# Four transformer layers on one core: in the two 16-head stages the transposes follow a group's scores by one step and the products with V by two, where they followed by two and three

## The chip, the cores and the metric

One core of one Trainium2 chip runs the whole program. The metric is the device time of one execution in microseconds (us). The engines are PE (TensorE, matrix products and transposes), DVE (VectorE), ACT (ScalarE), POOL (GpSimd) and SP (SyncE); each works through its own list of instructions in the order of the program, and they hand work over by semaphores. SBUF is the on-chip memory, PSUM the accumulator memory that PE writes to.

## The reference

Four layers, each an attention stage and a feed-forward stage, each followed by `x = layernorm(x + stage(x))`, on an input of 4 batches x 512 tokens x 128 features, all in fp32. The change touches the attention of layer 1 and of layer 2, both with 16 heads of 64 features:

```
# layer 1: 16 query heads, 4 key/value heads (each serves 4 query heads)
scores = einsum('bhqd,bhkd->bhqk', q, k) * 64 ** -0.5 + causal
probs  = softmax(scores);  out = einsum('bhqk,bhkd->bhqd', probs, v);  return out @ Wo.T

# layer 2: 16 heads, one more mask
S   = relu(att[:, 0]), shifted down by one query, without the first key and the diagonal
att = att - cumsum(S over queries)
att = where(keep, att, -inf)      # keep: the ~100 keys with the smallest sum, and the diagonal
y   = softmax(att) @ v;  return y @ W_proj.T + b_proj
```

The other stages (a one-head attention, a ternary gated feed-forward, a squared-relu feed-forward, two mixtures of experts, an attention over channels) are not touched.

## The kernel before

The four batches run in a hardware loop, one after the other; within a batch the eight stages follow each other. `A1` is the 16-head stage of layer 1 and `A2` that of layer 2; both use the same code (`heads_pe`, `heads_act`, `heads_dve`, `heads_pool`).

A stage first fills Q, K and V (L641 to L652). Then it goes through **groups**. A group is 128 queries (tile `i` of 4) and as many pairs of heads as make 512 columns of keys: query tile `i` sees `n = (i + 1) * 128` keys, so a group has one pair at 512 and at 384 keys, two pairs at 256 and four at 128. One head of a group is a **unit**. There are 22 groups in a stage: 8 with 512 keys, 8 with 384, 4 with 256 and 2 with 128. A1 takes the sizes in the order 384, 128, 256, 512, A2 in the order 512, 384, 128, 256.

The loop over `t` (L661, and the same loop on ACT and DVE) starts one group in each step and carries the earlier ones on. One group passes through:

- **scores** on PE (L669) into one of two PSUM buffers `GS`;
- **masks** on DVE (L793), one for each unit: add the mask, take the row minimum of the negated scores, write to one of four SBUF buffers `PRG`;
- **exp** on ACT (L758), one for each unit, with the row sums;
- **reciprocal** of the row sums on DVE (L800). It stands in the step after, behind the masks of the next group;
- **scaling** on POOL (L838), one instruction for each unit;
- **transposes** on PE (L711), of 128 x 128 blocks, into the one PSUM buffer `GX`. Those of a unit wait for its scaling (L708), and the first of a group for the copies that empty `GX` (L702 to L704). They stand `LX` steps behind the scores;
- **copies** out of `GX` into one of two buffers `PT`: in A1 half on ACT (L767) and half on DVE (L811), in A2 all on ACT (L769);
- **products with V** on PE (L727), `LO` steps behind the scores, and the copy of their result (L816 on DVE in A1, L774 on ACT in A2).

When the last group of a query tile is through, `heads_rows` multiplies by the output weights (L695) and the tile's normalization runs in the steps that follow; `self.step` takes the place of that from `LO` too. In A2, DVE also finds the keys to keep for the next query tile, in rounds of MAX8 and MATCH_REPLACE8 (L903 to L910), two rounds for each pair of heads of a step, behind the reciprocal.

So a step of PE is written

```
scores(t)                 # waits for the masks of t - 2
transposes(t - LX)        # waits for the scaling of t - LX and for the copies of the group before it
products with V(t - LO)   # waits for the copies of t - LO
```

Of the kernel before, what the change touches and what calls it, by code (L numbers as in the profile page):

```python
# [57 lines left out]
def transformer(nc, inp, out, last_stage=8):  # L58
    ctx = ExitStack()
    with ctx:  # L60
# [509 lines left out]
        GS = [psum[:, 0:2, :], psum[:, 2:4, :]]  # L570
        GX = psum[:, 4:6, :]
        GO = [psum[:, 6, :], psum[:, 7, :]]
        LX, LO = 2, 3

        class Group:

# [1089 lines left out]
```

## Time and profile before

| | us |
|---|---|
| median of 3 runs | 3670.2 |
| lowest and highest | 3670.17, 3671.58 |
| the profiled execution, its own time | 3670.1 |
| its span, first to last instruction | 3668.5 |
| PE busy | 3156.6 (86%) |
| DVE busy | 2364.9 (64%) |
| ACT busy | 1980.3 (54%) |
| POOL busy | 1393.8 (38%) |

A stage is read best from a stretch of the first batch: the loop over groups of A1 lies between 139 and 217 us, that of A2 between 265 and 371 us. The other three batches repeat them. In the view in order of time a row has the start, the busy time from the first to the last instruction of the row, the engine, the line, the shape, how many instructions were merged, and in brackets the idle time before it and who ended it. PEld rows are the weight loads of PE, which overlap its products. The granted clock is the share of TensorE's full 2.4 GHz that it was given; 0.50 is the lower of its two levels, 1.2 GHz.

### The profile page before, as it was taken

What the parts mean: (1) busy time and instruction counts of PE and PEld (TensorE: products, weight loads), DVE (VectorE), ACT (ScalarE), POOL (GpSimd) and SP (SyncE); (2) the same over time, 40 slices, a digit from 0 to 9 for tenths busy, and PEclk for the clock granted to TensorE, in tenths of its full rate; (3) what the DMA queues carried; (4) which work ended last, traced back from release to release, by engine and by line L of the source; (5) the groups of instructions that cost most, each with busy time, mean ns of one, the idle gap of its engine ahead of it and who ended that gap; (6) DMA issues with size and microseconds to landing.
All of it is one profiled execution on the core that took longest, in us unless ns stands there. A gap on an engine that the chain in (4) does not pass through costs nothing. (4 is left out here: it accounts for less than half of the span.)

```text
span 3668.5 us, 52722 instructions
## 1 busy us (share of the span) xinstructions
PE 3156.6 (86%) x19700; PEld 2207.3 (60%) x19700; DVE 2364.9 (64%) x4289; ACT 1980.3 (54%) x4488; POOL 1393.8 (38%) x1292
## 2 busy tenths in 40 slices
PE   4998998888799898888979889888897988988887
PEld 2556567776365646777536564677743655477773
DVE  3366379994246638999415653999931575499983
ACT  1546267773254528777226442877732654277763
POOL 0223066670031307766004120866501322177740
PEclk9998999999899998999989989999998999999999
DMA  4000100000200010000210001000011000100001
GB/s 131 1 1 1 49 12 1 1 1 24 69 1 1 1 61 1 1 1 1 61 33 1 1 1 61 1 1 1 1 61 33 1 1 10 52 1 1 1 1 63
DMA packets 69372, 68.51 MB, mean 19 GB/s; under 512 B 6077, under 2 KB 49623, under 8 KB 68970
## 3 DMA queue, kind: packets, MB, share of 16 engines
q1 hardware_dynamic: 60288, 56.15, 4.9%
q10 hardware_dynamic: 8810, 8.79, 0.7%
q8 instruction: 162, 2.65, 0.3%
q14 instruction: 112, 0.92, 0.1%
HBM read 63.88 MB, written 1.05 MB: 18 GB/s over the span
## 5 line engine op out<-in xcount | busy, mean ns | idle before, releaser
L1417 POOL TENSOR_TENSOR arena<-arena 128x1536 f32<-128x1536 f32 (+9 forms) x480 | 1020.0, 2155 | 395.6 <-DVE arena L1477 296.5
L1285 PE MATMUL psum<-ident,arena 128*128 128x128 f32 (+7 forms) x7168 | 870.0, 280 | 218.3 <-ACT arena L1386 218.1
L1285 PEld LDWEIGHTS psum<-ident,arena 128*128 128x128 f32 (+7 forms) x7168 | 795.8, 138 | 322.3 <-ACT arena L1386 278.6
L1376 ACT ACTIVATE arena<-arena 128x64 f32<-128x64 f32 (+7 forms) x2048 | 708.4, 486 | 139.4 <-PE psum L1294 139.4
L1477 DVE TENSOR_TENSOR arena<-arena,psum 128x1536 f32<-128x1536 f32 (+9 forms) x480 | 494.9, 1064 | 86.2 <-ACT arena L1386 78.5
L1463 DVE TENSOR_TENSOR arena<-arena,psum 128x1536 f32<-128x1536 f32 (+9 forms) x480 | 494.2, 1063 | 7.8 <-POOL arena L1417 5.8
L449 POOL TENSOR_SCALAR veps<-mv 128x1 f32<-128x1 f32 x128 | 24.7, 193 | 1192.4 <-DVE mv L444 1185.7
L838 POOL TENSOR_SCALAR arena<-arena 128x512 f32<-128x512 f32 (+3 forms) x512 | 265.0, 535 | 544.9 <-DVE arena L800 544.7
L1386 ACT ACTIVATE arena<-arena 128x1536 f32<-128x1536 f32 (+2 forms) x288 | 406.5, 1417 | 114.9 <-DVE arena L1463 114.9
L758 ACT ACTIVATE arena<-arena 128x512 f32<-128x512 f32 (+3 forms) x512 | 282.1, 553 | 209.8 <-DVE arena L793 209.8
L711 PE MATMUL psum<-ident,arena 128*128 128x128 f32 x1280 | 192.7, 294 | 92.9 <-ACT arena L769 63.5
L1063 PE MATMUL psum<-arena,stream 128*128 128x512 f32 x512 | 265.7, 601 | 5.0 <-DVE arena L1184 5.0
L711 PEld LDWEIGHTS psum<-ident,arena 128*128 128x128 f32 x1280 | 147.2, 148 | 191.7 <-ACT arena L769 103.2
L1080 PE MATMUL psum<-arena,stream 128*128 128x512 f32 x512 | 241.2, 595 | 0.0
L1294 PE MATMUL psum<-ident,arena 128*128 128x128 f32 (+7 forms) x2048 | 234.0, 273 | 0.0
L1180 DVE TENSOR_TENSOR arena<-arena,psum 128x512 f32<-128x512 f32 x128 | 88.1, 688 | 215.3 <-PE psum L1080 215.3
L1294 PEld LDWEIGHTS psum<-ident,arena 128*128 128x128 f32 (+7 forms) x2048 | 223.4, 137 | 1.2
L1112 ACT ACTIVATE arena<-psum 128x512 f32<-128x512 f32 x128 | 76.4, 597 | 266.3 <-PE psum L1080 266.3
L1184 DVE TENSOR_TENSOR arena<-arena 128x512 f32<-128x512 f32 x128 | 88.6, 692 | 172.5 <-ACT arena L1114 172.5
L669 PE MATMUL psum<-arena 64*128 64x256 f32 (+3 forms) x1024 | 189.8, 477 | 9.6 <-DVE arena L793 7.7
L793 DVE CUSTOM_DVE_ANT_0 arena<-psum,cmask 128x384 f32<-128x384 f32 (+3 forms) x256 | 112.0, 488 | 119.9 <-PE psum L669 119.9
L727 PE MATMUL psum<-arena 128*64 128x128 f32 x2560 | 186.4, 288 | 0.4
(212 smaller groups left out, 4234.1 us busy)
## 6 DMA issues: line engine op xcount, KB each, us to landing
stream<-in_L_ffn_W SPq DMA_DIRECT2D x160, 256.0 KB, 3.1
arena<-in_L_ffn_h_w SPq DMA_DIRECT2D x8, 1024.0 KB, 8.4
arena<-in_L_ffn_w_w SPq DMA_DIRECT2D x12, 256.0 KB, 4.7
arena<-in_L_ffn_h_w ACTq DMA_DIRECT2D x2, 1024.0 KB
wa<-in_L_attn_W_attn ACTq DMA_DIRECT2D x1, 1536.0 KB
wq<-in_L_attn_Wq ACTq DMA_DIRECT2D x2, 512.0 KB
wo<-in_L_attn_Wo ACTq DMA_DIRECT2D x2, 512.0 KB
x<-in_L_attn_x SPq DMA_DIRECT2D x4, 256.0 KB, 3.7
```

What stands on the lines that cost most here:

```text
L711: last = nc.tensor.transpose(GX[:, half, c:c + P], two(PRG[b % 4])[:, half, c:c + P], ident[:])
L758: nc.scalar.activation(pr, pr, ACT.Exp, bias=nb[:, u:u + 1], scale=-1.0, accum_out=rsum[:, u:u + 1]).then_inc(s["probs"], 1)
L838: nc.gpsimd.tensor_scalar(pr, pr, rinv[:, u:u + 1], 1.0, ALU.mult, ALU.mult).then_inc(s["scaled"], 1)
L1063: nc.tensor.matmul(psO, slot[:, 2 * HID + m * P:2 * HID + (m + 1) * P], HR[n % 3], start=n == 0, stop=top2 and n == NE * NM - 1).then_inc( ...
L1080: nc.tensor.matmul(up_bank(n, j), slot[:, j * HID + m * P:j * HID + (m + 1) * P], XS[e % 2], start=True, stop=True).then_inc(s["up"], 1)
L1285: last = nc.tensor.matmul(ps[ch.half][0:rows, to:to + P], buf[:, c:c + rows], ident[:], start=first, stop=False, is_transpose=True, skip_g ...
L1294: last = nc.tensor.matmul(ps[0][0:rows, 0:P], EA[:, k * NH * OWN:k * NH * OWN + rows], ident[:], start=False, stop=k == HD - 1, is_transpo ...
L1376: nc.scalar.activation(by_key[:, 0:HD - r, j], keys[:, h, 0:HD - r], ACT.Exp, bias=NB[:, j:j + 1], scale=Q3[tt % 2][:, j:j + 1]).then_inc( ...
L1386: nc.scalar.activation(D3[n % 5][:, 0:cols], D3[n % 5][:, 0:cols], ACT.Exp).then_inc(s["e"], 1)
L1417: last = nc.gpsimd.tensor_tensor(of_piece(D3[n % 5], piece), q, keys_on(K3[tt % 2], k, nk, w), ALU.mult)
L1463: last = nc.vector.tensor_tensor(d, d, queries_on(psM[ch.half], ch, piece), ALU.subtract)
L1477: last = nc.vector.tensor_tensor(of_piece(W3[n % 2], piece), of_piece(D3[n % 5], piece), keys_on(psV, k, nk, w), ALU.mult)
```

## The change

Both distances of the loop are made one step shorter. The copies out of `GX` and of the results, the steps of `heads_rows` and of the normalization (`self.step`), and the end of the loop (`A.ng + LO`) take their places from the same two numbers and move with them. Nothing is added or removed; every instruction of a group is the same.

```diff
@@ -570,7 +570,7 @@
         GS = [psum[:, 0:2, :], psum[:, 2:4, :]]
         GX = psum[:, 4:6, :]
         GO = [psum[:, 6, :], psum[:, 7, :]]
-        LX, LO = 2, 3
+        LX, LO = 1, 2
 
         class Group:
```

On PE, at the start of the loop of A1, before the change (`a1_scaled` counts scaled units, `a1_pt` and `a1_pt_dve` the two copies, `a1_masked` masks):

```order
L669 MATMUL psum<-arena 128x384 x3
L669 MATMUL psum<-arena 128x384 [waits a1_masked]
L669 MATMUL psum<-arena 128x384
L711 MATMUL psum<-ident,arena 128x128 [waits a1_scaled]
L711 MATMUL psum<-ident,arena 128x128 x2
L711 MATMUL psum<-ident,arena 128x128 [waits a1_scaled]
L711 MATMUL psum<-ident,arena 128x128 x2
L669 MATMUL psum<-arena 128x384 [waits a1_masked]
```

The same place in the changed kernel:

```order
L669 MATMUL psum<-arena 128x384 x3
L711 MATMUL psum<-ident,arena 128x128 [waits a1_scaled]
L711 MATMUL psum<-ident,arena 128x128 x2
L711 MATMUL psum<-ident,arena 128x128 [waits a1_scaled]
L711 MATMUL psum<-ident,arena 128x128 x2
L669 MATMUL psum<-arena 128x384 [waits a1_masked]
L669 MATMUL psum<-arena 128x384
```

The transposes of the first group stood behind the scores of the third group, and now stand behind those of the second; the scores of the third group follow them.

On DVE, the same stretch of A1, as a difference (`-` before, `+` after; `ISA` rows are the masks and the reads of their minimum):

```order
 L793 ISA arena 128x1
 L800 RECIPROCAL arena<-arena 128x2
-L793 ISA arena<-psum,cmask 128x384
-L793 ISA arena 128x1
-L793 ISA arena<-psum,cmask 128x384
-L793 ISA arena 128x1
-L800 RECIPROCAL arena<-arena 128x2
 L811 COPY arena<-psum 128x384
```

The copy of the first group's transposes came behind the masks of the third group and the reciprocal of the second; it now comes directly behind the reciprocal of the first group, ahead of the third group's masks.

## Rows read from the trace of the kernel before

**Rows 1.** The page, busy time of each engine: share of span, instructions

```profile
PE 3156.6 (86%) x19700; PEld 2207.3 (60%) x19700; DVE 2364.9 (64%) x4289; ACT 1980.3 (54%) x4488; POOL 1393.8 (38%) x1292
```

**Rows 2.** Busy time by stretch (length, busy per engine, granted clock, DMA): A1, A2

```profile
139.00:217.00 78.00, 73.12 (x682) 52.37 (x682) 52.82 (x205) 49.69 (x157) 35.39 (x70) 1.00 0.01 2
264.80:371.00 106.20, 86.04 (x694) 61.49 (x692) 72.08 (x293) 61.64 (x175) 35.31 (x70) 0.86 0.00 1
```

**Rows 3.** Line L711: what ended the idle time before it (us, times)

```profile
  ACT arena L769: 166.7, 118
```

**Rows 4.** In order of time: a step of A1 with 512 keys

```profile
188.39 1.09 PE L711 MATMUL psum<-ident,arena 128*128 128x128 f32 x8
188.51 0.69 DVE L793 CUSTOM_DVE_ANT_0 arena<-psum,cmask 128x512 f32<-128x512 f32 x1 [0.18 <-PE psum L669]
...
189.42 1.09 PE L727 MATMUL psum<-arena 128*64 128x128 f32 x16
...
189.99 1.36 POOL L838 TENSOR_SCALAR arena<-arena 128x512 f32<-128x512 f32 x2 [1.74 <-DVE arena L800]
...
191.62 0.69 DVE L793 CUSTOM_DVE_ANT_0 arena<-psum,cmask 128x512 f32<-128x512 f32 x1 [0.63 <-PE psum L669]
```

**Rows 5.** In order of time: POOL hands the first scaled unit of A1 to PE

```profile
142.63 2.34 POOL L838 TENSOR_SCALAR arena<-arena 128x384 f32<-128x384 f32 x4 [17.14 <-DVE arena L800]
...
143.27 1.12 PE L711 MATMUL psum<-ident,arena 128*128 128x128 f32 x6 [0.84 <-POOL arena L838]
```

**Rows 6.** In order of time: a step of A1 with 384 keys

```profile
147.74 0.56 DVE L793 CUSTOM_DVE_ANT_0 arena<-psum,cmask 128x384 f32<-128x384 f32 x1 [0.55 <-PE psum L669]
...
148.43 0.88 PE L727 MATMUL psum<-arena 128*64 128x128 f32 x12
...
148.96 1.15 POOL L838 TENSOR_SCALAR arena<-arena 128x384 f32<-128x384 f32 x2 [1.31 <-DVE arena L800]
...
150.20 0.56 DVE L793 CUSTOM_DVE_ANT_0 arena<-psum,cmask 128x384 f32<-128x384 f32 x1 [0.55 <-PE psum L669]
```

**Rows 7.** In order of time: from 128 keys to 256 keys in A1

```profile
160.52 0.29 DVE L793 CUSTOM_DVE_ANT_0 arena<-psum,cmask 128x128 f32<-128x128 f32 x1 [0.20 <-PE psum L669]
...
162.50 2.82 POOL L838 TENSOR_SCALAR arena<-arena 128x128 f32<-128x128 f32 x8 [1.59 <-DVE arena L800]
...
164.56 0.42 DVE L793 CUSTOM_DVE_ANT_0 arena<-psum,cmask 128x256 f32<-128x256 f32 x1 [0.77 <-PE psum L669]
```

**Rows 8.** In order of time: a step of A1 with 256 keys

```profile
173.78 0.42 DVE L793 CUSTOM_DVE_ANT_0 arena<-psum,cmask 128x256 f32<-128x256 f32 x1 [2.58 <-PE psum L669]
...
175.43 1.85 POOL L838 TENSOR_SCALAR arena<-arena 128x256 f32<-128x256 f32 x4 [3.68 <-DVE arena L800]
...
176.89 0.42 DVE L793 CUSTOM_DVE_ANT_0 arena<-psum,cmask 128x256 f32<-128x256 f32 x1
```

**Rows 9.** In order of time: masks of A2 with 512, 384 and 128 keys

```profile
286.79 0.69 DVE L793 CUSTOM_DVE_ANT_0 arena<-psum,arena 128x512 f32<-128x512 f32 x1
...
290.57 0.69 DVE L793 CUSTOM_DVE_ANT_0 arena<-psum,arena 128x512 f32<-128x512 f32 x1
...
303.80 0.56 DVE L793 CUSTOM_DVE_ANT_0 arena<-psum,arena 128x384 f32<-128x384 f32 x1 [0.48 <-DVE arena L906]
...
306.66 0.56 DVE L793 CUSTOM_DVE_ANT_0 arena<-psum,arena 128x384 f32<-128x384 f32 x1 [0.45 <-DVE arena L906]
...
323.11 0.29 DVE L793 CUSTOM_DVE_ANT_0 arena<-psum,arena 128x128 f32<-128x128 f32 x1 [1.33 <-issue]
...
332.72 0.29 DVE L793 CUSTOM_DVE_ANT_0 arena<-psum,arena 128x128 f32<-128x128 f32 x1
```

**Rows 10.** Clock: two stretches as in Rows 2, and PE's rows behind long waits

```profile
738.00:752.00 14.00, 8.76 (x77) 7.86 (x75) 13.90 (x13) 13.55 (x29) 7.39 (x5) 1.00 0.00 1
334.00:353.00 19.00, 14.21 (x72) 11.53 (x72) 9.35 (x44) 9.77 (x34) 7.45 (x20) 0.50 0.01 2
...
647.83 2.84 PE L1285 MATMUL psum<-ident,arena 128*128 128x128 f32 x24 [2.23 <-ACT arena L1386]
337.00 1.97 PE L711 MATMUL psum<-ident,arena 128*128 128x128 f32 x8 [6.87 <-ACT arena L769]
```

## Prediction, written before the changed kernel was run

> **What bounds the kernel now.** I read the page's busy times first: PE is busy for 86% of the span [rows 1], so any time that PE stands still in a stretch that it bounds is time of the kernel. Then the two stretches by engine: A1's loop takes 78.0 us with PE busy for 73.1 of them, so PE bounds A1. A2's loop takes 106.2 us, with PE busy for 86.0 and DVE for 72.1 [rows 2]; there the rounds on DVE set the pace in part.
>
> Then the steps in order of time. I measure a step from the first mask of a group to the first mask of the next. In A1 a step with 512 keys takes 191.62 - 188.51 = 3.11 us [rows 4], one with 384 keys 150.20 - 147.74 = 2.46 us [rows 6], one with 256 keys 3.11 us [rows 8], and the step from 128 keys to the next size 4.04 us [rows 7]. In A2 a step with 512 keys takes 3.78 us, with 384 keys 2.86 us, and the first one with 128 keys 9.61 us [rows 9]: DVE has two rounds for each pair of heads there.
>
> What the reader is to see in rows 4: POOL starts to scale a group 1.48 us after the first mask **of the next group** (189.99 - 188.51), since the reciprocal stands behind those masks. So the scaling of a group is done one whole step late, and the transposes on PE stand far enough back to find it ready. Where PE does wait ahead of them, it is for ACT's copy (166.7 us over the whole kernel for L769, [rows 3]), and not for POOL.
>
> **The change, part by part.** No instruction is added or removed. What changes is where PE stands in its list. Written for step t, PE now has scores(t), transposes(t-1), products with V(t-2), scores(t+1). The scaling of t-1 waits for the reciprocal of t-1, which waits on DVE for the masks of t, which wait for scores(t). And scores(t+1) stand behind the transposes of t-1 on PE. That closes a loop over a single step through four engines. Everything queued behind the waiting transposes pays: the products with V, the scores of the next group, thus DVE's next masks, thus ACT's exps. In A1 DVE also waits in its own list for its half of the copies (L811) and the result (L816), but these end ahead of the scores that follow, so they add nothing.
>
> The length of the loop, for 512 keys:
>
> - first mask of t to the start of POOL on t-1: 1.48 us [rows 4];
> - POOL's two units, 1.36 us [rows 4], and the handover to PE. The handover is 143.27 - 142.63 = 0.64 us for a first unit of 2.34 / 4 = 0.585 us, so 0.06 us [rows 5]. Together 1.42 us;
> - the transposes of the first unit run while POOL scales the second. The four of the last unit are left: eight take 189.42 - 188.39 = 1.03 us [rows 4], so 0.13 us each and 0.51 us;
> - products with V and the next scores, up to the next first mask: 191.62 - 189.42 = 2.20 us [rows 4].
>
> The sum is 1.48 + 1.42 + 0.51 + 2.20 = **5.61 us, where a step takes 3.11 us** in A1 (+2.50) and 3.78 us in A2 (+1.83, since DVE's rounds fit into POOL's and PE's part of the loop).
>
> For 384 keys: 148.96 - 147.74 = 1.22; 1.15 + 0.06; three transposes 0.39; 150.20 - 148.43 = 1.77 [rows 6]. Sum 4.59 us: +2.13 in A1, +1.73 in A2 (2.86 now, [rows 9]).
>
> For 256 keys: 175.43 - 173.78 = 1.65; 1.85 + 0.06 [rows 8]; two transposes 0.26; 2.20 as for 512 keys. Sum 6.02 us: +2.91.
>
> For 128 keys: 162.50 - 160.52 = 1.98; 2.82 + 0.06 [rows 7]; one transpose 0.13; about 2.0, between 1.77 and 2.20. Sum 6.99 us: +2.95 over the 4.04 us in A1. In A2 the step takes 9.61 us on DVE alone [rows 9], longer than the loop, so +0; that cover is lost only if the loop grows by 2.6 us.
>
> Sums for one batch. A1: 8 x 2.50 + 8 x 2.13 + 4 x 2.91 + 2 x 2.95 = 54.5, less 2.1 for the first step, which has no group to transpose: **52.4 us**. A2: 8 x 1.83 + 8 x 1.73 + 4 x 2.91 + 0 = 40.1, less 1.8 for the first step: **38.3 us**. The three `heads_rows` blocks are on PE's path now and stay there: 0. The end of a stage has one turn of the loop fewer, but its last group must go through the whole chain in either kernel; I take 0 (bounds: one step of 2.5 us less, or 2.5 us more, for 8 stages 20 us either way). Where PE waits for ACT's copy now [rows 3] it will wait for POOL instead; that wait is inside the old step and so inside the difference.
>
> Four batches: 4 x (52.4 + 38.3) = **363 us**.
>
> **The clock** is the unknown. In the new step PE idles from the end of the scores to the first transposes: 5.61 us less the 3.1 us of its work leaves about 2.3 us in one piece. The trace shows both outcomes. Where bursts of 2.84 us alternate with waits, PE is busy for only 8.76 of 14.0 us and the granted clock stays 1.00; one such wait is 2.23 us long [rows 10]. Behind a wait of 6.87 us the clock was at the lower level (0.50, 1.2 GHz), and it stayed there for 19 us, 14.2 of them with PE busy [rows 10]. A step at the lower clock costs 1.97 instead of 1.09 us for eight transposes [rows 10, 4], nearly double; on the loop, half of the transposes and the 2.20 us of products and scores double, so +0.5 + 1.9 = 2.4 us. A2 has two such low stretches today (its mean is 0.86, [rows 2]); now each step in them pays. I take the row nearest to the new pattern, the recurring wait with clock 1.00, for the bulk, and 4 low steps for each batch (two at the start of A2, two around its 128-key groups): 4 x 4 x 2.4 = 38 us. The ends: 0 low steps (0 us) and half of all 44 steps of a batch (4 x 22 x 2.4 = 211 us).
>
> **Sum.** The profiled execution took 3670.1 us, 1.6 us over its span and 0.1 us from the median of 3670.2 us. 3670.1 + 363 + 38 = 4071 us.
>
> **A rule that is weighed.** The Trainium skill, page "TensorE: Matmul & The Clock Gate", section "HAM oscillation — how this bites in real kernels", describes a kernel with some 2 us of products and a wait of 3 to 5 us for each tile, where the clock falls again in every tile. By that rule, taken to hold for our 2.3 us too, nearly all steps would be low, and the sum would be 3670 + 363 + 4 x 44 x 2.4 = 4455 us. The trace agrees for the long wait [rows 10] and disagrees for the recurring waits of 2.2 us, which are shorter than the page's.
>
> **The rivals.**
>
> *The clock falls in many steps of both stages.* The idle piece of 2.3 us is a little longer than any that the trace shows at clock 1.00, and the steps with 128 and 256 keys have transposes that come one by one behind POOL, which leaves PE nearly idle for longer. For it: A2's stretches at 0.50. Against: the stretch at 738 us. At half of the steps: 3670 + 363 + 211 = 4244 us. Chance 0.24.
>
> *Only A1 pays.* DVE's rounds cover the loop in A2, so that A2 stays at its pace: 3670 + 4 x 52.4 = 3880 us. It would need POOL to be ready within 3.78 us including the products and scores; the legs sum to 5.61. Chance 0.07.
>
> *Not slower.* The transposes of t-1 find their scaling ready, the waits for ACT's copy go, and each stage ends a turn earlier. This decides at one place, the reciprocal on DVE: if it were issued ahead of the masks of the next group, or if those masks and POOL (1.48 + 1.42 us) fit beside PE's own work between two scores. Then the price is 8 stages x one step of 2.5 to 3.1 us less: 3670 - 8 x 2.8 = 3648 us. Against it: the trace shows POOL starting 1.48 us after the next group's mask in every step, and PE has nothing but the waiting transposes in front of it. Chance 0.02. That the change doesn't do what it says (a distance that is also fixed elsewhere) would give 3670 us; the order of the program shows it moved. Chance 0.01.
>
> **How the numbers follow.** The forecast, 4071 us, has 0.66. Its own bounds are the end of the stages (20 us either way) and the low steps (from 0 to about 10 for each batch): 4010 to 4150 us. The range has to reach into the first rival, up to 4240 us, and leaves out the milder cases, for 8 in 10: 3990 to 4240 us. A measurement of this kernel can tell about 0.2% from no change. Faster by more than that: 0.02; within it: 0.01; slower: 0.97.
>
> **What would show it.** In the profile after: PE's idle time ahead of L711 ended by POOL (L838), and hardly by ACT's copies; steps of 5.6 us with 512 keys and 4.6 us with 384 keys in both stages, 6.0 and 7.0 us with 256 and 128 keys; A1's loop near 130 us, A2's near 150 us; all engines' busy times as now but for PE's at the lower clock; the other six stages unchanged. The forecast is wrong if the steps show other lengths at clock 1.00 (a leg is mis-sized), if the granted clock in A1 falls below 0.9 (the first rival), or if A2's steps with 512 keys stay at 3.8 us (the second).

## The result: 605 us slower, and the profile after

The changed kernel takes **4275.1 us** (median of 3 runs, 4272.6 to 4275.3) where the kernel before takes 3670.2 us. The ratio is 1.165, 95% interval 1.162 to 1.167. The forecast was 4071 us with a range up to 4240 us. The direction and the loop of one step hold; the share of the clock does not.

The granted clock over the span in 40 slices (tenths), before:

```profile
PEclk9998999999899998999989989999998999999999
```

The page after, first the busy times and then the same 40 slices:

```profile
PE 3459.5 (81%) x19700; PEld 2385.4 (56%) x19700; DVE 2369.8 (55%) x4289; ACT 2008.0 (47%) x4488; POOL 1391.5 (33%) x1292
...
PEclk9788799999878779999987878999998686899999
```

DVE and POOL are busy for as long as in [rows 1], ACT for 28 us more. PE is busy for 303 us **more** (3459.5 against 3156.6) with the same 19700 products: it ran them slower. The two 16-head stages of the first batch by stretch, which answer to [rows 2] (length, busy times, then the granted clock as the third number from the end):

```profile
141.00:302.00 161.00, 111.82 (x673) 76.05 (x674) 53.78 (x203) 51.81 (x155) 35.20 (x70) 0.71 0.00 1
351.20:526.00 174.80, 120.04 (x710) 82.25 (x708) 72.98 (x296) 66.95 (x179) 36.00 (x72) 0.72 0.00 1
```

A1's loop took 78 us and takes 161, A2's took 106 and takes 175, and the mean clock fell from 1.00 and 0.86 to 0.71 and 0.72. These two differences make 152 us for a batch and 606 us for four: all of the loss of 605 us lies in the two stages.

What ended the idle time ahead of the transposes, after (line L711, us and times), where [rows 3] had ACT's copy:

```profile
  issue: 505.3, 168
  POOL arena L838: 494.1, 411
```

The copy is gone from the list and POOL is there, as the loop of one step demands. This view, like [rows 3], counts the weight loads of PE together with its products, so its times are not PE's lost time. The products alone stand in the page, before and then after:

```profile
L711 PE MATMUL psum<-ident,arena 128*128 128x128 f32 x1280 | 192.7, 294 | 92.9 <-ACT arena L769 63.5
...
L711 PE MATMUL psum<-ident,arena 128*128 128x128 f32 x1280 | 296.2, 378 | 413.0 <-POOL arena L838 412.4
```

They waited 412.4 us for POOL after the change, and 63.5 us (not 166.7) for ACT's copy before it. In order of time, a step of A1 with 384 keys after, to set beside [rows 6]:

```profile
161.35 0.56 DVE L793 CUSTOM_DVE_ANT_0 arena<-psum,cmask 128x384 f32<-128x384 f32 x1 [1.29 <-PE psum L669]
...
162.57 1.15 POOL L838 TENSOR_SCALAR arena<-arena 128x384 f32<-128x384 f32 x2 [5.42 <-DVE arena L800]
...
163.30 1.51 PE L711 MATMUL psum<-ident,arena 128*128 128x128 f32 x6 [2.00 <-POOL arena L838]
...
164.74 1.55 PE L727 MATMUL psum<-arena 128*64 128x128 f32 x12
...
166.22 1.65 PE L669 MATMUL psum<-arena 64*128 64x384 f32 x4
...
167.92 0.56 DVE L793 CUSTOM_DVE_ANT_0 arena<-psum,cmask 128x384 f32<-128x384 f32 x1 [1.29 <-PE psum L669]
```

The loop is readable leg by leg: masks, 1.22 us later POOL, 0.73 us later the transposes (with 2.00 us of idle time on PE before them), the products with V, the next scores, the next masks. The step is 167.92 - 161.35 = 6.57 us, where the sum of legs gave 4.59. The first two legs are as forecast. All the difference is on PE: twelve passes of products take 1.55 us instead of 0.88, the scores 1.65 instead of 0.92. This is the lower of the two clock levels, 1.2 GHz, and it held through this whole stretch (length, busy times, clock 0.50):

```profile
146.00:176.00 30.00, 20.46 (x95) 11.87 (x93) 9.56 (x34) 8.58 (x24) 4.88 (x9) 0.50 0.00 1
```

With 512 keys the clock changes inside each step. A step after, beside [rows 4]:

```profile
283.20 0.69 DVE L793 CUSTOM_DVE_ANT_0 arena<-psum,cmask 128x512 f32<-128x512 f32 x1 [0.77 <-PE psum L669]
...
285.53 1.94 PE L711 MATMUL psum<-ident,arena 128*128 128x128 f32 x8 [2.37 <-POOL arena L838]
...
287.40 1.70 PE L727 MATMUL psum<-arena 128*64 128x128 f32 x16
...
289.03 1.13 PE L669 MATMUL psum<-arena 64*128 64x512 f32 x4
...
290.20 0.69 DVE L793 CUSTOM_DVE_ANT_0 arena<-psum,cmask 128x512 f32<-128x512 f32 x1 [0.77 <-PE psum L669]
```

Behind 2.37 us of idle time the transposes run at the lower level (1.94 us for eight, 1.09 in [rows 4]), and the clock is back for the scores (1.13 us). This step is 7.00 us long. Its neighbours take 7.12 to 7.26 us, and the one that carries the product with the output weights 9.20 us.

### The profile page after: what moved, and what is told of

The parts are those of the page before. It is cut to its first block and busy times, and to the rows that moved or that the text cites. A ratio compares the mean times of both kernels' runs of the same rounds, so it can differ in the third digit from the quotient of the medians.

```text
span 4273.5 us, 52722 instructions
## 1 busy us (share of the span) xinstructions
PE 3459.5 (81%) x19700; PEld 2385.4 (56%) x19700; DVE 2369.8 (55%) x4289; ACT 2008.0 (47%) x4488; POOL 1391.5 (33%) x1292
## 5 line engine op out<-in xcount | busy, mean ns | idle before, releaser
L1285 PE MATMUL psum<-ident,arena 128*128 128x128 f32 (+7 forms) x7168 | 867.4, 279 | 209.4 <-ACT arena L1386 208.2
L1285 PEld LDWEIGHTS psum<-ident,arena 128*128 128x128 f32 (+7 forms) x7168 | 792.0, 137 | 313.7 <-ACT arena L1386 268.0
L711 PE MATMUL psum<-ident,arena 128*128 128x128 f32 x1280 | 296.2, 378 | 413.0 <-POOL arena L838 412.4
L711 PEld LDWEIGHTS psum<-ident,arena 128*128 128x128 f32 x1280 | 193.6, 183 | 590.1 <-issue 505.3
L793 DVE CUSTOM_DVE_ANT_0 arena<-psum,arena 128x512 f32<-128x512 f32 (+3 forms) x256 | 112.6, 488 | 350.5 <-PE psum L669 182.8
L727 PE MATMUL psum<-arena 128*64 128x128 f32 x2560 | 289.7, 397 | 0.4
L727 PEld LDWEIGHTS psum<-arena 128*64 128x64 f32 x2560 | 228.1, 206 | 49.0 <-issue 47.6
L669 PE MATMUL psum<-arena 64*128 64x256 f32 (+3 forms) x1024 | 251.6, 614 | 1.9 <-ACT arena L745 1.9
```

Of the source, the lines that this page charges most:

```text
L711: last = nc.tensor.transpose(GX[:, half, c:c + P], two(PRG[b % 4])[:, half, c:c + P], ident[:])
L727: last = nc.tensor.matmul(bank[half * HD:(half + 1) * HD, j * P:(j + 1) * P], V[:, c:c + HD], pt[:, half, j * g.n + kt * P:j * g.n + (kt + ...
L1285: last = nc.tensor.matmul(ps[ch.half][0:rows, to:to + P], buf[:, c:c + rows], ident[:], start=first, stop=False, is_transpose=True, skip_g ...
```

## The experiments

Two causes are proposed for the loss of 605 us. The first is the **loop of one step**: transposes wait for a scaling that starts behind the next group's masks. The second is the **low clock** that PE's idle piece brings. A rival to the first is that the products with V, or the copies, are what hurts. A rival to the second is that I undersized a leg. Unless said otherwise, each kernel below has the changed distances 1 and 2.

### near_fill: the same loop at the full clock

```diff
+                    fill(pe, A, t, 10)     # 8 for 384 keys; 26, 34, 28 in three long waits of A2
                     heads_transpose(pe, A, t - LX)
...
+        def fill(pe, A, t, times):
+            bank = GO[0]
+            if t >= LO:
+                A.bank_free(pe, "values", t - LO)
+                bank = A.bank("values", t - LO)
+            for _ in range(times):
+                nc.tensor.matmul(bank[:, 0:P], ident[:], ident[:], start=True, stop=True)
```

> The changed kernel (distances 1 and 2) with 128x128 products of the identity put into PE's wait ahead of the transposes, 10 for a step (8 for 384 keys, 26 to 34 where DVE's rounds make the wait long), into the result bank that is free then. They do no work for the output. If the missing 204 us of the forecast are the clock, its steps run at 5.6 us (512 keys) and 4.6 us (384 keys) at a granted clock near 1.00 and the time is the sum of the legs, 3670 + 363 = 4033 us (4000 to 4060). If the steps are long for another reason (a leg that I sized too small), the fill only adds work and the time stays at 4275 us or above.

The idle products go ahead of the transposes, 10 in most steps. Measured: **4042.0 us**, 233 us less than the changed kernel though PE has more to do. The stretches of the two stages:

```profile
141.00:270.00 129.00, 127.87 (x1082) 98.34 (x1079) 53.65 (x203) 50.48 (x154) 35.19 (x70) 1.00 0.01 1
321.00:463.00 142.00, 140.32 (x1205) 112.21 (x1202) 70.40 (x289) 66.04 (x175) 35.27 (x70) 1.00 0.01 1
```

The clock is 1.00 in both, and a step with 512 keys in A1 (here L802 are the masks, L693 the fill, L847 POOL, L720 the transposes, L736 the products):

```profile
247.20 2.50 PE L693 MATMUL psum<-ident 128*128 128x128 f32 x20
247.32 0.69 DVE L802 CUSTOM_DVE_ANT_0 arena<-psum,cmask 128x512 f32<-128x512 f32 x1 [0.51 <-PE psum L669]
...
248.80 1.36 POOL L847 TENSOR_SCALAR arena<-arena 128x512 f32<-128x512 f32 x2 [4.32 <-DVE arena L809]
...
249.64 1.23 PE L720 MATMUL psum<-ident,arena 128*128 128x128 f32 x8
...
250.80 1.09 PE L736 MATMUL psum<-arena 128*64 128x128 f32 x16
...
253.00 0.69 DVE L802 CUSTOM_DVE_ANT_0 arena<-psum,cmask 128x512 f32<-128x512 f32 x1 [0.77 <-PE psum L669]
```

The step is 253.00 - 247.32 = 5.68 us where the sum of legs gave 5.61. With 384 keys it is 4.66 us (4.59), with 256 keys 6.12 (6.02), from 128 keys to the next size in A1 7.08 (6.99). So no sum of legs was more than 0.10 us too small, and filling the waits, which brings the clock to 1.00, is worth 233 us.

### x1_o3 and x2_o2: one distance at a time

Against the kernel before:

```diff
-        LX, LO = 2, 3
+        LX, LO = 1, 3      # x1_o3
+        LX, LO = 2, 2      # x2_o2
```

> Only the transposes one step nearer (distance 1), the products with V at 3 as before. My theory: the loop of a single step is closed by the transposes, which wait for the scaling behind the next group's masks, so nearly the whole loss is here: 4250 to 4300 us, POOL ending PE's waits. Rival: the products with V are what hurts, as they now follow their transposes by one step in a shorter pipeline; then this stays near 3670 us.

Measured: **4259.6 us**. The transposes alone bring 589 of the 605 us, with the same release (line L711, weight loads counted in) and nearly the same clock in A1 as the changed kernel, 0.74 where that has 0.71:

```profile
  POOL arena L838: 503.6, 428
...
141.00:300.00 159.00, 109.21 (x673) 74.72 (x672) 51.68 (x203) 50.60 (x154) 35.17 (x70) 0.74 0.00 1
```

The first steps of this kernel show something else. With 384 keys and the same idle piece of 2.0 us, the transposes ran at the full clock at first and at the lower one later:

```profile
151.69 1.01 PE L711 MATMUL psum<-ident,arena 128*128 128x128 f32 x6 [2.00 <-POOL arena L838]
...
168.53 1.51 PE L711 MATMUL psum<-ident,arena 128*128 128x128 f32 x6 [1.99 <-POOL arena L838]
```

> Only the products with V one step nearer (distance 2), the transposes at 2 as before. The products of a group then stand right behind its own transposes and wait for the copies out of PSUM, which wait for the transposes' end and, on ACT, for the exps of that step. My estimate from the legs: a step with 512 keys becomes masks, exps and the 0.6 to 1.0 us copy, then products and scores, 5.0 us in A1 and 5.4 us in A2: 3960 us at full clock, up to 4030 us with low steps. If only the transposes' distance matters, 3670 us.

Measured: **4052.5 us**, 22 us above the upper figure. A step with 512 keys in A1 is 4.99 us, as estimated. Its wait is another one: the products with V follow their own transposes and wait for ACT's copy, which stands behind that step's exps.

```profile
240.78 0.69 DVE L793 CUSTOM_DVE_ANT_0 arena<-psum,cmask 128x512 f32<-128x512 f32 x1 [0.51 <-PE psum L669]
...
243.58 1.09 PE L727 MATMUL psum<-arena 128*64 128x128 f32 x16 [1.81 <-ACT arena L767]
...
245.78 0.69 DVE L793 CUSTOM_DVE_ANT_0 arena<-psum,cmask 128x512 f32<-128x512 f32 x1 [0.77 <-PE psum L669]
```

The clock was 0.92 in A1's stretch, but 0.79 in A2's (141 to 262 and 313 to 463 us). That this is what I had too small is likely, but no run fills this kernel's waits.

Each distance by itself costs a lot, 589 and 381 us, and together they cost 605. The 381 us are no part of the 605. They come from products that stand in the same step as their own transposes. In the changed kernel the products are one step behind them, as before, and the page has PE waiting 0.4 us in all ahead of L727. So the products' distance, with the transposes already at 1, adds only the last 16 us.

### near_recip_first: the place where the loop closes

```diff
             for t in range(A.ng + LO):
+                if 0 <= t - 1 < A.ng:
+                    g = A.groups[t - 1]
+                    dve.wait_ge(s["probs"], g.end)
+                    nc.vector.reciprocal(rinv[:, g.u0:g.end], rsum[:, g.u0:g.end]).then_inc(s["rinv"], 1)
                 if t < A.ng:
...
-                if 0 <= t - 1 < A.ng:
-                    g = A.groups[t - 1]
-                    dve.wait_ge(s["probs"], g.end)
-                    nc.vector.reciprocal(rinv[:, g.u0:g.end], rsum[:, g.u0:g.end]).then_inc(s["rinv"], 1)
```

> The changed kernel (1 and 2), but on DVE the reciprocal of group t-1 stands ahead of the masks of group t. If the loop is closed through that reciprocal's place behind the next masks, scaling starts before those masks and a step shrinks to about 4 us in A1 and to DVE's 3.8 us in A2 (512 keys): 3790 us (3740 to 3850), clock above 0.9. If the loss came from PE's own order or from the copies, moving the reciprocal does little: above 4150 us.

Measured: **3794.3 us**. Moving one small instruction of DVE gives back 481 of the 605 us, the clock's part included: the mean clock is 0.95 and 0.87 in the two stages (139 to 238 and 285 to 402 us). In A1 with 512 keys (L785 is the reciprocal, L797 the masks):

```profile
214.21 0.13 DVE L785 RECIPROCAL arena<-arena 128x2 f32<-128x2 f32 x1
...
214.64 0.69 DVE L797 CUSTOM_DVE_ANT_0 arena<-psum,cmask 128x512 f32<-128x512 f32 x1 [0.30 <-PE psum L669]
...
215.30 1.36 POOL L838 TENSOR_SCALAR arena<-arena 128x512 f32<-128x512 f32 x2
...
216.14 1.23 PE L711 MATMUL psum<-ident,arena 128*128 128x128 f32 x8 [1.54 <-POOL arena L838]
```

POOL starts 0.66 us after the masks instead of 1.48, and here only that late because it had the normalization's two instructions first; in the next step it starts 0.34 us ahead of them. The remaining 124 us over the kernel before were not taken apart. PE still waits for POOL, 1.54 us in the last row and 150.3 us in all ahead of the products of L711.

### near_fill_small_pool: POOL's leg by itself

Against near_fill; two idle products fewer in most steps go with it, and the kernel leaves out most of the scaling:

```diff
-                        nc.gpsimd.tensor_scalar(pr, pr, rinv[:, u:u + 1], 1.0, ALU.mult, ALU.mult).then_inc(s["scaled"], 1)
+                        nc.gpsimd.tensor_scalar(pr[:, 0:16], pr[:, 0:16], rinv[:, u:u + 1], 1.0, ALU.mult, ALU.mult).then_inc(s["scaled"], 1)
```

> near_fill with POOL scaling only the first 16 columns of each unit, so most probabilities stay unscaled (work left out), and 2 idle products fewer for a step. This measures POOL's leg of the loop. POOL's unit falls from 0.68 us (512 keys) to about 0.26 us; the transposes of the last unit then no longer wait for it. By the sum of legs a step with 512 keys falls by 0.6, with 384 by 0.5, with 256 by 0.8 us, some 25 us for a batch: 3940 us (3920 to 3970). If POOL were not in the loop, the time would stay at near_fill's 4042 us.

Measured: **3943.7 us**, 98 us below near_fill, 3940 expected. POOL's line in near_fill, then in this kernel (busy us, mean ns of one):

```profile
L847 POOL TENSOR_SCALAR arena<-arena 128x512 f32<-128x512 f32 (+3 forms) x512 | 264.1, 532 | 886.8 <-DVE arena L809 886.4
```

```profile
L847 POOL TENSOR_SCALAR arena<-arena 128x16 f32<-128x16 f32 x512 | 133.5, 278 | 912.2 <-DVE arena L809 911.8
```

POOL works 131 us less in all, and 98 of them come off the time, of an engine that is busy for a third of the span. Steps with 512, 384 and 256 keys in A1 are 5.10, 4.19 and 5.31 us, so 0.58, 0.47 and 0.81 us shorter; 0.6, 0.5 and 0.8 were expected.

### near_fill_half and near_fill_2: how much fill the clock needs

Against near_fill, with `times` for its numbers:

```diff
-                    fill(pe, A, t, times)
+                    fill(pe, A, t, times // 2)      # near_fill_half
+                    fill(pe, A, t, times // 4)      # near_fill_2
```

> Distances 1 and 2 with half as many idle products as near_fill (5 for a step, 4 for 384 keys), so that PE's idle piece of a step is about 1.2 us instead of 2.3 us. If the length of the idle piece decides, the clock stays near 1.00 and the time is that of near_fill or a little less, 4035 us. If any recurring idle piece of this kind brings the low clock, it lies between: 4100 to 4200 us.

Measured: **4041.6 us**, the same as with all of the fill, with idle pieces of 1.06 us (512 keys) and 0.91 us (384 keys). The stretches (the second one holds some 28 us around A2 as well):

```profile
141.00:270.00 129.00, 107.07 (x869) 75.63 (x866) 53.62 (x203) 50.43 (x154) 35.38 (x70) 0.99 0.00 1
310.00:480.00 170.00, 142.72 (x1071) 103.19 (x1070) 88.28 (x340) 74.38 (x191) 36.19 (x72) 0.96 0.00 1
```

> Distances 1 and 2 with a quarter of near_fill's idle products (2 for a step), which leaves PE's idle piece at about 1.9 us where near_fill_half left 1.2 us and the changed kernel 2.4 us. near_fill_half kept a clock of 0.96 to 0.99 in these stages. If 1.9 us is short enough, as the recurring waits of 1.5 to 2.2 us in the channel stage are, the time is again 4040 us; if it is already too long, the time lies between 4040 and 4275 us, near 4200 us.

Measured: **4143.2 us**, between. This kernel shows both levels, by size of group. With 384 keys the idle piece is 1.35 us and the clock stays at 1.00; around the groups with 128 keys it is 2.09 us and the transposes run at the lower level (1.51 us for six); with 512 keys it is 1.73 us, and there are steps of both kinds:

```profile
161.24 1.01 PE L720 MATMUL psum<-ident,arena 128*128 128x128 f32 x6 [1.35 <-POOL arena L847]
...
176.21 1.51 PE L720 MATMUL psum<-ident,arena 128*128 128x128 f32 x6 [2.09 <-POOL arena L847]
...
249.63 1.23 PE L720 MATMUL psum<-ident,arena 128*128 128x128 f32 x8 [1.73 <-POOL arena L847]
250.79 1.67 PE L736 MATMUL psum<-arena 128*64 128x128 f32 x16
252.39 2.08 PE L669 MATMUL psum<-arena 64*128 64x512 f32 x4
...
262.52 1.23 PE L720 MATMUL psum<-ident,arena 128*128 128x128 f32 x8 [1.73 <-POOL arena L847]
263.68 1.09 PE L736 MATMUL psum<-arena 128*64 128x128 f32 x16
264.70 1.13 PE L669 MATMUL psum<-arena 64*128 64x512 f32 x4
```

The same piece of 1.73 us is followed by slow scores (2.08 us) once and by fast ones (1.13 us) twelve microseconds later. So the length of the idle piece alone does not decide, as in x1_o3 above; what else does is open. That waits of up to 2.2 us keep the clock, as they do in the channel stage, does not carry over to these stages.

### before_fill and before_fill_long: the kernel before with its own low stretches filled

The diff of before_fill; before_fill_long has 19 in place of the 9, and 3 in the step behind:

```diff
+                    fill(pe, A, t, {2: 14, 17: 5, 18: 29, 19: 9}.get(t, 0) if A is A2 else 0)
                     heads_transpose(pe, A, t - LX)
```

> The kernel before (distances 2 and 3) with 58 of the same idle products in A2 alone: 14 ahead of the first group's transposes, 5, 29 and 9 in the three steps around its 128-key groups, where PE waits for DVE's rounds. If A2's two low stretches cost time there (a delay of the masks by 0.8 us and 5 to 6 us in the rows and steps behind the 128-key groups), each batch gains about 6 us: 3646 us (3640 to 3660). If DVE hides the low clock in A2, nothing changes: 3670 us.

Measured, with 57 idle products and not 58: **3658.8 us**, ratio to the kernel before 0.9967, interval 0.9954 to 0.9979. It is faster, but by half of what was expected. A2's stretch, to set beside [rows 2], where its clock was 0.86:

```profile
264.80:371.00 106.20, 93.74 (x830) 70.47 (x829) 73.88 (x299) 62.23 (x178) 36.07 (x72) 0.98 0.01 1
```

The masks of A2 span 87.3 us instead of 90.4, so 3.2 us for each batch come back and not 6. The 0.8 us at the first groups came as expected (a step of 4.54 us is 3.78). Behind the 128-key groups 2.3 us came (12.00 to 9.67 us), where 5 to 6 were expected.

> before_fill with 19 idle products instead of 9 in the step behind A2's 128-key groups and 3 in the next, since PE still idled for 2.1 us there and the clock fell again. If that low stretch still costs rows and products, another 1 to 3 us for each batch: 3650 us (3645 to 3658). If the longer fill delays the transposes by as much, it stays at 3659 us.

Measured: **3657.5 us**, ratio 0.9963 (0.9948 to 0.9977), not to be told from before_fill. The step that was to gain fell from 9.67 to 8.30 us, but the next one grew from 3.11 to 3.83 us. The clock of A2's stretch is 1.00 now, and the masks span 86.6 us. So all of A2's low clock cost its masks 3.8 us for a batch; where the rest of the expected 6 us was hidden was not looked into.

## Why the prediction was wrong

From the first group's first mask to the last group's first mask of a stage in the first batch, in us, from DVE's rows of each trace:

| | A1 | A2 | sum | x 4 batches, over before |
|---|---|---|---|---|
| before | 65.8 | 90.4 | 156.3 | |
| forecast by the legs | | | 247.0 | 363 |
| near_fill (clock 1.00) | 117.8 | 128.7 | 246.5 | 361 |
| after | 147.9 | 157.8 | 305.7 | 598 |

**What bounds the kernel; the loop: right.** POOL ended PE's waits ahead of the transposes, the masks came 1.22 and 1.49 us before POOL as read from [rows 4, 6], DVE's 128-key steps in A2 stayed at DVE's pace (9.63 us after, 9.61 in [rows 9]), and the channel stage kept its pace (the page has its transposes of L1285 busy for 867.4 us, 870.0 before).

**The legs: right.** 363 us were forecast, 361 us are there at the full clock, and near_fill's time is 371 us above the kernel before. That the two numbers are so close is partly luck. In A2 the steps with 384 keys paid 15.5 us where 13.8 were forecast, those with 256 keys 9.5 where 11.6 were. Of the remaining 10 us, 8 lie between A1's last masks and A2's first: 62.8 us in near_fill, 60.9 before. The prediction put the ends of the stages at 0, with bounds of 20 us.

**The clock: the term that was mis-sized.** The step of the forecast that failed reads "I take the row nearest to the new pattern, the recurring wait with clock 1.00, for the bulk, and 4 low steps for each batch". I had 38 us there; it is 4275 - 4042 = 233 us. The prediction's own sign was there too: the clock in A1 was to stay above 0.9, and was 0.71. Two errors partly cancel. Of the 42 steps between masks in a batch, 38 are at least 0.9 us longer than in near_fill, where I had 4 low ones. But a touched step costs less than the 2.4 us that I took: 7.00 to 7.26 instead of 5.68 us with 512 keys, some 1.4 us, since the clock is back before the scores, and 6.57 instead of 4.66, so 1.9 us, with 384 keys. The row from the channel stage did not carry over. In its stretch at clock 1.00 [rows 10] PE has only transposes, in bursts of up to 2.84 us, behind waits of 1.48 to 1.95 us:

```profile
741.16 2.84 PE L1285 MATMUL psum<-ident,arena 128*128 128x128 f32 x24 [1.95 <-ACT arena L1386]
745.48 2.84 PE L1285 MATMUL psum<-ident,arena 128*128 128x128 f32 x24 [1.48 <-ACT arena L1386]
750.12 2.15 PE L1285 MATMUL psum<-ident,arena 128*128 128x128 f32 x17 [1.80 <-ACT arena L1386]
```

In A1, a stretch with pieces of 2.0 us between bursts of transposes and products stayed at 0.50 for 30 us. What makes the difference is not shown.

**The rivals.** The first, a low clock in many steps, is what happened. I had priced it at 4244 us with half of the steps low at 2.4 us each, and gave it 0.24; the result is 31 us above that. The upper end of the range stopped 4 us short of this rival's own point, with nothing above it, so the bound that I had worked out (all 44 steps, 4455 us) was cut off: the range was too narrow by its own reasoning. The second, only A1 pays, did not come: A2 paid 67 us for a batch to A1's 82. The third, not slower, named the place of the reciprocal as what decides. Moving it gave back 481 us, but the kernel was then still 124 us slower than before, where this rival had 3648 us; so that place is most of the loss and not all of it.

**The rule that was weighed.** The Trainium skill, page "TensorE: Matmul & The Clock Gate", section "HAM oscillation — how this bites in real kernels", gives a wait of 3 to 5 us in each tile for a clock that falls again every time. These runs agree with the pattern, at shorter waits: with 512 keys the clock fell and rose in each step behind 2.37 us. By that rule the sum was 4455 us, with every step low at 2.4 us. Measured are 4275 us: nearly every step was low, but for some 1.6 us each (59 us more than near_fill for a batch, over 38 steps).

## What to carry to other kernels

Before shortening the distance between pipeline stages, follow the data once around through every engine's program order: here a reciprocal that stands behind the next group's masks made each step as long as the whole chain, and PE, which bounds the stage, then waited for POOL, which is busy for a third of the time. Then price the idle piece that appears on PE twice, once as time and once as clock. Keep the second bound in the range unless a row of the same pattern excludes it. Where PE must wait in every step, a few idle products in a free PSUM bank are cheap: five in most steps gave back all of the clock's 233 us, and 57 well-placed ones made the kernel before 0.33% faster.

## What was not expected of the hardware

- A recurring idle piece of 2.0 us in steps of 6.57 us held PE at its lower level for 30 us of a stretch in which it was busy for 20.46 us. The slower products lengthen the step but not the idle piece, and this did not bring the clock back.
- In steps with 512 keys the clock fell and rose once in each step of 7.1 us: 1.94 us for eight transposes behind 2.37 us of idle time, 1.13 us for the scores 3.5 us later.
- The same idle piece was followed by either level in one stage of one run: 1.73 us with 512 keys (near_fill_2), 2.0 us with 384 keys (x1_o3).
- In the channel stage of the kernel before, transposes alone, behind waits of 1.48 to 1.95 us, had clock 1.00 for 14 us.
